# A four-layer vision network on one core: weights scaled later, heads loaded earlier, norms reordered, and GRU inputs in two fp16 parts

## The reference, cut to what matters

```python
# layer 0: retention (12 heads of 8 channels)
x = x + dwconv3x3(x)
xn = layer_norm(x, ln1_g, ln1_b)
o = softmax(rotate(xn @ q_w) @ rotate(xn @ k_w * scaling).T + mask) @ (xn @ v_w)
x = x + ((o + dwconv5x5(v)) @ out_w + out_b)
h = gelu(layer_norm(x, ln2_g, ln2_b) @ fc1_w + fc1_b)
x = x + ((h + dwconv3x3(h)) @ fc2_w + fc2_b)

# layer 1: four GRUs over the 1024 tokens of an image (two forward, two backward)
xn = layer_norm(x, ln_g, ln_b)
x_inner, z = split(xn @ w_in.T)            # 192 and 192 channels
def step(hprev, gxt):                      # gxt = x_inner @ wih.T + bih
    gh = hprev @ whh.T + bhh
    r = sigmoid(gxt[:, :h] + gh[:, :h])
    z = sigmoid(gxt[:, h:2*h] + gh[:, h:2*h])
    n = tanh(gxt[:, 2*h:] + r * gh[:, 2*h:])
    return (1 - z) * n + z * hprev
x = x + (silu(sum of the GRUs) * silu(z)) @ w_out.T

# layers 2 and 3: norm, projection, 3x3 convolution, four decaying scans,
# norm, projection, norm, MLP; twice
```

## Time and profile before

| what | value |
|---|---|
| median of three runs | 3178.32 us (3177.25 to 3181.61) |
| the profiled execution's own time | 3182.78 us |
| its span in the trace | 3181.1 us |
| busy over the span: PE, PE weight loads, DVE | 2994.2, 2308.5, 2536.2 us |
| busy over the span: ACT, POOL | 1746.1, 1063.9 us |
| mean granted TensorE clock | 0.722 of full speed |

### The profile page before, as it was taken

How to read it: one execution, slowest core, us unless ns; L and a number is a source line. 1 busy time by engine, 2 the same in 40 slices (tenths; PEclk the granted TensorE clock), 3 DMA queues, 4 the chain that set the end, 5 groups by cost and what they waited for, 6 DMA issues and landing times. The chain is left out here.

```text
span 3181.1 us, 127160 instructions
## 1 busy us (share of the span) xinstructions
PE 2994.2 (94%) x50436; PEld 2308.5 (73%) x50436; DVE 2536.2 (80%) x12120; ACT 1746.1 (55%) x5568; POOL 1063.9 (33%) x2520
## 2 busy tenths in 40 slices
PE   6799999999969989999999999999999999789987
PEld 3365665556624459999999999999999999366654
DVE  6799999999956678888888888888888888688772
ACT  2599999999912244444444444444444444344443
POOL 2377787777710022222222222222222222000000
PEclk8899999999989965555555555555555555689998
DMA  2323233232230000000000000000000000000000
GB/s 64 97 92 118 93 117 118 91 118 96 84 91 20 12 2 4 4 4 4 4 4 4 4 4 4 4 4 4 4 4 4 4 4 4 1 1 1 1 6 15
DMA packets 48219, 104.75 MB, mean 33 GB/s; under 512 B 11306, under 2 KB 18794, under 8 KB 47693
## 3 DMA queue, kind: packets, MB, share of 16 engines
q1 hardware_dynamic: 31308, 42.78, 4.8%
q0 software_dynamic: 13824, 50.34, 4.4%
q10 hardware_dynamic: 2560, 4.35, 0.5%
HBM read 84.06 MB, written 13.37 MB: 31 GB/s over the span
## 5 line engine op out<-in xcount | busy, mean ns | idle before, releaser
L578 PE MATMUL g_zr<-g_hp,g_wp 97*128 97x4 f16 x24576 | 1070.6, 171 | 3.3 <-DVE g_hp L630 3.3
L578 PEld LDWEIGHTS g_zr<-g_hp,g_wp 97*128 97x128 f16 x24576 | 945.2, 107 | 87.9 <-DVE g_hp L630 4.9
L668 ACT ACTIVATE g_e<-g_n 96x8 f32<-96x8 f32 x2048 | 355.4, 174 | 562.2 <-DVE g_n L617 562.2
L630 DVE TENSOR_TENSOR_SCAN g_hp<-g_gates,g_e 96x16 f16<-96x16 f32 x2048 | 383.8, 187 | 258.6 <-ACT g_e L668 179.4
L556 PE MATMUL g_zr<-s_inner,g_wi 96*128 96x64 bf16 (+1 forms) x6144 | 571.2, 234 | 3.1 <-DVE g_hs L605 3.1
L665 ACT ACTIVATE g_gates<-g_zr 96x16 f32<-96x16 f32 x2048 | 397.9, 194 | 243.5 <-PE g_zr L578 243.5
L585 PE MATMUL g_n<-g_hp,g_wp 97*128 97x8 f16 x8192 | 520.2, 174 | 0.0
L938 DVE CUSTOM_DVE_ANT_0 a_negated<-a_scores,a_mask 128x1024 f32<-128x1024 f32 x384 | 468.3, 1220 | 62.3 <-PE a_scores L856 61.8
L964 ACT ACTIVATE a_probs<-a_negated,a_negmax 128x1024 f32<-128x1024 f32 x384 | 442.3, 1152 | 18.4 <-DVE a_negmax L938 8.7
L886 PEld LDWEIGHTS a_turned<-a_ident,a_probs 128*128 128x128 f32 x3072 | 357.8, 141 | 93.7 <-ACT a_probs L964 3.5
L617 DVE TENSOR_TENSOR_SCAN g_n<-g_gates,g_n 96x24 f32<-96x24 f32 x2048 | 422.4, 206 | 2.3 <-ACT g_gates L665 2.3
(11 more groups left out here) (317 smaller groups left out, 3513.7 us busy)
## 6 DMA issues: line engine op xcount, KB each, us to landing
a_mask<-in_L_mask POOLq DMA_DIRECT2D x96, 512.0 KB, 5.3
a_k<-k_rows SPq DMA_DIRECT2D x96, 144.0 KB
a_q<-q_rows SPq DMA_DIRECT2D x96, 72.0 KB
o_parts<-a_o_sb SPq DMA_DIRECT2D x384, 18.0 KB
o_part<-o_parts SPq DMA_DIRECT2D x16, 192.0 KB
o_part<-o_parts ACTq DMA_DIRECT2D x16, 192.0 KB
q_rows<-r_parts SPq DMA_DIRECT2D x12, 192.0 KB
k_rows<-r_parts SPq DMA_DIRECT2D x4, 576.0 KB, 3.6
```

Of the source, the lines that this page charges most:

```text
L578: mm = pe.matmul(zr_bank[u, k][:, 1 - g, d, :, at], wp[0:97, part, (2 * u + d) * NG + g, :], hp[u][0:97, d * NB:(d + 1) * NB, e], start=False,
L630: ve.tensor_tensor_scan(flat(hp[u][0:C]), keep, flat(e1[u][:, :, :]), 0.0, ALU.mult, ALU.subtract).then_inc(h1_ok[u], 1)
L668: act.activation(e1[u][:, :, 0], tn[u, k][:, :, 2], ACT.Tanh, scale=to_tanh).then_inc(n_and_zh[u], 1)
```

## The change

Four things are changed at once.

The **norms** get an order in which image 3's mean and centring come earlier; `factor` is a list of tiles, so that images 1 and 2 spread into the mean's tiles and no longer wait for the scaling of the image before. The second and third shifts move behind the roots.

The **inputs of the GRUs** are split in two fp16 parts in place of three bf16 parts, and `PRODUCTS` has 3 pairs in place of 6. So that fp16's range does, the input is scaled by a power of two `of_x`, found in `down_and_gates` from the norm's gain and offset and the sizes of `w_in`; the weights' scale takes the largest input weight into account too. The recurrent weights keep their two fp16 parts.

The **weights of layers 2 and 3** are scaled (`ema.scale_weights`) at the start of the recurrence block, ahead of `scan_matrices`, and no longer ahead of the split.

The **parts of image 0** are loaded at the end of attention, into the four `first_masks` buffers, ahead of the last three groups' stores in SP's queue; these buffers live until the joining is done, and the joining loads images 1 to 3 alone.

```diff
 layernorm:
+        factor = [factor, mean[0], mean[1], factor]
             def spread_out(b):
                 pe.wait_ge(split, 4 * (b + 1))
-                if b:
-                    pe.wait_ge(scaled, b)
+                if b in (1, 2):
+                    pe.wait_ge(centered, b + 2)
+                if b == 3:
+                    pe.wait_ge(scaled, 1)
...
             average_of(2)
             variance_of(0)
+            average_of(3)
             variance_of(1)
             spread_out(0)
-            average_of(3)
             variance_of(2)
...
             invert(0)
+            centre(3)
             invert(1)
             scale(0)
-            centre(3)
             invert(2)
...
             root(1)
-            shift(0)
             square(3)
             root(2)
+            shift(0)
+            root(3)
             shift(1)
-            root(3)
             shift(2)
             shift(3)

-PRODUCTS = ((0, 0), (0, 1), (1, 0), (1, 1), (0, 2), (2, 0))
+PRODUCTS = ((0, 0), (0, 1), (1, 0))
+REACH = 9.85

 down_and_gates, ScalarE:
-            act.activation(magnitude, whole, ACT.Abs).then_inc(absolute, 1)
+            act.activation(gain_size[:, :], gates["gain"][:, :], ACT.Abs).then_inc(absolute, 1)
+            act.activation(offset_size[:, :], gates["offset"][:, :], ACT.Abs).then_inc(absolute, 1)
+            act.activation(w_in_size[:, :], w_in[:, 0:2 * C], ACT.Abs).then_inc(absolute, 1)
+            act.activation(magnitude[0][0:C + 1], whole, ACT.Abs).then_inc(absolute, 1)
+            act.activation(magnitude[1][:, :, :], wih[1][:, :, :], ACT.Abs).then_inc(absolute, 1)
+            act.wait_ge(magnitude_read, 1)
+            act.activation(magnitude[0][0:C], wih[0][:, :, :], ACT.Abs).then_inc(absolute, 1)
...
-            for k in range(2):
-                act.wait_ge(rest0, k + 1)
-                act.activation(wi[0:K[k], k, 1, :, 0:C], rests[k][:, :, :], ACT.Copy).then_inc(part1, 1)
 TensorE:
+                        pe.wait_ge(reached, 1)
+                        for m in range(2):
+                            mm = pe.matmul(bound[:, m:m + 1], w_in_size[:, m * C:(m + 1) * C], reach[:, :],
+                                           start=(m == 0), stop=True, skip_group_check=True)
+                        mm.then_inc(bounded, 1)
+                    if b == 0 and k == 1:
+                        pe.wait_ge(reduced, 3)
...
 VectorE:
+            ve.tensor_reduce(row_max[0:C + 1, 0:1], magnitude[0][0:C + 1], AX.XY, ALU.max).then_inc(magnitude_read, 1)
+            ve.tensor_reduce(row_max[:, 1:2], magnitude[1][:, :, :], AX.XY, ALU.max).then_inc(reduced, 1)
+            ve.tensor_reduce(row_max[0:C, 3:4], bound, AX.X, ALU.max).then_inc(reduced, 1)
+            ve.tensor_reduce(row_max[0:C, 2:3], magnitude[0][0:C], AX.XY, ALU.max).then_inc(reduced, 1)
+            add(0)
...
+            add(2)
             for k in range(2):
                 ve.wait_ge(part0, k + 1)
-                ve.tensor_tensor(rests[k][:, :, :], wih[k][:, :, :], wi[0:K[k], k, 0, :, 0:C],
-                                 ALU.subtract).then_inc(rest0, 1)
-            add(2)
-            for k in range(2):
-                ve.wait_ge(part1, k + 1)
-                ve.tensor_tensor(wi[0:K[k], k, 2, :, 0:C], rests[k][:, :, :], wi[0:K[k], k, 1, :, 0:C], ALU.subtract)
+                ve.tensor_tensor(wi[0:K[k], k, 1, :, 0:C], wih[k][:, :, :], wi[0:K[k], k, 0, :, 0:C], ALU.subtract)

 gru_phase, VectorE:
+            ema.scale_weights(ve)
             ema.scan_matrices(ve)

 attention, SP:
             heads(sp, body)
+            sp.wait_ge(maxed, (NH - 1) * CHUNKS_PER_HEAD + 16)
+            sp.wait_ge(o_out[0], 64 * (NH * GROUPS_PER_HEAD // 2 - 1))
+            for half in range(2):
+                for j in range(4):
+                    sp.dma_start(first_parts[j][:, half, :], o_parts[:, half, 0, j, 0:8, :]).then_inc(first_parts_in, 16)

 joining of the heads:
-                for b in range(NB):
+                for b in range(1, NB):
                     for j in range(4):
-                        eng.dma_start(part[b][:, j, half, :], o_parts[:, half, b, j, 0:8, :]).then_inc(loaded[b], 16)
+                        eng.dma_start(part[b][j][:, half, :], o_parts[:, half, b, j, 0:8, :]).then_inc(loaded[b], 16)
...
+                first_half(0)
                 ve.wait_ge(norm_in, 16 * 2 * NB)

 project_and_split, ScalarE:
-                    act.activation(parts(h, b)[0], product[h][:, :], ACT.Copy).then_inc(part0, 1)
-                for h in range(2):
-                    act.wait_ge(rest0, 2 * b + h + 1)
-                    act.activation(parts(h, b)[1], y[:, h, cols(b)], ACT.Copy).then_inc(part1, 1)
+                    act.activation(parts(h, b)[0], product[h][:, :], ACT.Identity, scale=by).then_inc(part0, 1)
 GpSimd:
-            po.memset(inner[C:C + 2, 1, 0, :, :], 1.0)
-            po.memset(inner[C:C + 2, 1, 1:3, :, :], 0.0)
+            po.memset(inner[C:C + 2, 1, 0, :, :], 1.0).then_inc(ones_ok, 1)
+            po.memset(inner[C:C + 2, 1, 1, :, :], 0.0)
+            po.wait_ge(ones_ok, 1)
+            po.tensor_scalar(inner[C:C + 2, 1, 0, :, :], inner[C:C + 2, 1, 0, :, :], of_x[C:C + 2, 0:1].bitcast(F), None,
+                             ALU.mult)
 VectorE:
-            ema.scale_weights(ve)
...
-                    ve.tensor_tensor(y[:, h, cols(b)], product[h][:, :], parts(h, b)[0],
-                                     ALU.subtract).then_inc(rest0, 1)
-                for h in range(2):
-                    ve.wait_ge(part1, 2 * b + h + 1)
-                    ve.tensor_tensor(parts(h, b)[2], y[:, h, cols(b)], parts(h, b)[1], ALU.subtract)
+                    ve.scalar_tensor_tensor(parts(h, b)[1], product[h][:, :], by, parts(h, b)[0], ALU.mult,
+                                            ALU.subtract).then_inc(split, 1)
```

More of the change, by code:

```diff
@@ L1314, in retention_block @@
                             lepe, lepe_w)
-        attention(nc, d["L0_mask"], first_masks, first_mask_in, q_rows, k_rows, vt, o_parts, vpad, lepe, lepe_w)
-        values.close()
+        first_parts = [t[0:C, :].rearrange("c (f t) -> c f t", f=2) for t in first_masks]
+        attention(nc, d["L0_mask"], first_masks, first_mask_in, q_rows, k_rows, vt, o_parts, first_parts, first_parts_in,
+                  vpad, lepe, lepe_w)
         gates = gate_tiles(nc, gates_ctx)
+        gates.update(gain=v["L1_ln_g"], offset=v["L1_ln_b"])
         recycle(nc)
@@ L1323, in retention_block @@
             sem = lambda name: ctx.enter_context(semaphore(nc, "o_" + name))
-            part = [sb(f"part{b}", [C, 4, 2, BANK]) for b in range(NB)]
+            later_parts = {b: sb(f"part{b}", [C, 4, 2, BANK]) for b in range(1, NB)}
+            part = [first_parts] + [[later_parts[b][:, j] for j in range(4)] for b in range(1, NB)]
             total = [sb(f"total{i}", [C, 2, BANK]) for i in range(2)]
@@ L1451, in project_and_split @@
         product = [ctx.enter_context(nc.psum_tensor(f"s_in_product{m}", [C, L], F)) for m in range(4)]
-        ready, part0, rest0, part1, gated = map(sem, ("in_ready", "part0", "rest0", "part1", "gated"))
+        ready, part0, split, gated, ones_ok = map(sem, ("in_ready", "part0", "split", "gated", "ones_ok"))
+        by = of_x[0:C, 0:1].bitcast(F)
         block = ctx.enter_context(nc.Block())
-        parts = lambda h, b: [inner[0:C, h, p, b, T:T + L] for p in range(3)]
+        parts = lambda h, b: [inner[0:C, h, p, b, T:T + L] for p in range(2)]
         @block.tensor
```

149 lines of the change are left out of this document (93 added, 56 removed).

## The result

Beside runs of the kernel before on the same chip, the changed kernel took 3144.84 us (median of 4, 3138.49 to 3149.84) where the kernel before took 3179.97 (median of 4): a ratio of 0.9889, 95% interval 0.9868 to 0.9910, about -35 us. A second comparison on another occasion gave 3151.15 us (5 runs) beside 3179.35 (19 runs): 0.9916, interval 0.9903 to 0.9928, about -28 us. The forecast was -26.3. One program thus gave 7 us more on one occasion than on the other, and the two intervals overlap only between 0.9903 and 0.9910. The profile of the first comparison is of its shortest run (3138.49 us, span 3136.8), so a second profile of each kernel stands beside it.

The account below looks back on a forecast made before the run. It took the recurrence's loop, not TensorE, as the bound there, and block savings elsewhere as going straight into the span: -10.0 + 1.0 - 13.2 - 5.0 + 0.3 + 0.6 = -26.3, from 3178.32 to 3152.0 us, range 3144 to 3159.

Parts of the forecast that it names:

- Rival (a): Recurrence: TensorE is the bound, so 4608 fewer projections give -226 us, about 2926; chance 2%.
- (b): Recurrence: sparser projections make state matmuls restart from idle; at 0.05 us a step the time is 3203; chance 2%.
- Split, -10.0: Split of the input: without the scaling, VectorE starts early and TensorE runs through; gain 10.0 us.
- Rival (c): Split: GpSimd's work holds VectorE after all, gain 0 to 5 in place of 10, 3157 to 3162; chance 8%.
- Scaling at the start, +1.0: Start of the recurrence: twelve small VectorE instructions, 3.4 us against 2.3 of cover; cost 1.0 us with a semaphore.
- Norms, -13.2: Three norms: new order keeps VectorE busy; gains 4.5, 4.5 and 4.2 us, ends -11 and -15.
- The run-through: Norms: the new order worked through with the trace's durations, 16.0 us from first inverse to end of last shift.
- Early heads, -5.0: Joining of the heads: image 0's parts already there, TensorE's last groups setting the end; gain 5.0, worst 3, best 7.
- The term of one drawn-out VectorE addition (+0.8): Joining: VectorE's sum of the last image's parts slowed because GpSimd's ran first, counted once, +0.8.
- Rival (d): Joining bound by TensorE, so early loads give nothing, and third norm stays at the low clock: 3158; chance 10%.
- (e): The change does not do what it says, its form being norms at half their gain: 3158; chance 3%.
- Gates' weights, +0.6: Gates' weights block: TensorE stops once about 0.4 us, plus two tiny products; cost 0.6, ends 0 and +3.

Follow-up runs that it names:

- the three parts timed alone: The kernel before with one part each: norms' new order, ratio 0.9936; first image's parts loaded early, 0.9988; small weights scaled at the recurrence's start, 0.9956.
- the missing products: The kernel before with three of the six products left out, still of bf16, the output lacking their share: ratio 0.9972.

## Why the prediction was right, point by point

The forecast of 3152.0 us was 7 over the first median and 1 over the second. All blocks came out near their forecast size, but the joining did so in part by luck.

- **What bounds the recurrence.** The step that carried the most, that TensorE's 100 of 100 us is no limit, held: half the projections gone, the period was 1.5113 and 1.5135 us, and with them gone alone 1.5135, where the kernel before has 1.5133 and 1.5140. Rival (a), -226 us, is out, and (b) as well. Of the rule of the Trainium skill that I had weighed there (Perfetto Trace Analysis, Identifying the Most-Contended Engine) I used one half, weight-load busy time; the page names it together with MFU, the share of the peak FLOP/s, which I didn't work out. The half that I used would have misled: weight loads fell from 94.63 to 84.52 of 100 us and the step hardly changed.
- **Split, -10.0: -9.6.** The pause was the scaling, and the scaling was held by the memset, shown by four kernels (the scaling moved, the memsets held, the two-input form, the scaling put back). Rival (c), that GpSimd's work holds the subtraction, is out; the product took 10.99 us (12 estimated). What I had not seen is why one instruction was held and its neighbours were not.
- **Scaling at the start, +1.0: +0.84.** As worked out. But my sentence that TensorE being ready earlier is of no use was true only of this placement: with the scaling elsewhere the fewer projections give 2.5 there against the kernel before, and 3.0 if some matrices go too.
- **Norms, -13.2: -13.8.** The run-through gave 16.0 us from first inverse to end, the trace 15.97. In the third the saving was 4.9 by the means of the pairs, but that leans on the one norm of before whose fold ran at 1.2 GHz; over all seven profiles of either order (means 26.7 and 22.4) it is 4.3, close to the 4.2 taken.
- **Early heads, -5.0: -5.9 (-6.8 alone).** The size was near, the path to it was not. I read waits for the loads off the first two images and let TensorE's last groups set the end. In the kernel before, VectorE already worked without a gap from 907.14 on, and in the changed one it does so from its first multiplication, while TensorE's last projection waits for VectorE (0.51 and 1.38 us). The 7.1 us between landings was also the first gap alone: in the same profile GpSimd's later additions, which start as the parts land, follow after 6.1 and 5.3. The term of one drawn-out VectorE addition (+0.8) fell on GpSimd in one profile and on VectorE in the other. Landings still set part of the end in two of the seven profiles with the early loads (38.9 and 40.8 us), where image 2's parts came 8.3 and 8.4 us after image 1's and VectorE then waited 2.7 us for GpSimd's addition. Over the seven joinings with the old loads (40.7 to 47.8 us) and the seven with the new (35.6 to 40.8) the means differ by 5.8, but the spread within each is 5 to 7. Attention's +0.3 can't be seen in its 804 to 809 us. Rival (d) is out, and so is (e), which had the norms at half their gain.
- **Gates' weights, +0.6: +0.8.**
- **The error that the range needed.** The bounds of "recurrence +-1" and "medians +-2" were too narrow. The period's level is worth up to 5.4 us, the last layers 8.7, by execution, and 10.7 us of the first profile's gain lie in these two. The first median came out at 3144.84, at the edge of the range, and that it stayed inside is luck; that the same spread moved this median is likely, but a profile shows one execution alone.

Open: the three parts timed alone and the missing products come by their ratios to -20, -4, -14 and -9 us, and by their blocks to -11.6, -6.8, -8.2 and -2.5; three of the four are larger than their blocks, and together they are larger than the whole change. Whether a program's own layout favours a level of the period I could not tell from one profile each.

## What to carry to other kernels

An engine that is busy for all of a stretch may only be filling someone else's wait: look for the one place where the filling is missing, and compare the pace. Before GpSimd is given a long memset or product, look at which of VectorE's instructions beside it are of the quick one-input form in SBUF (here the scalings, not the reductions); a 0.3 us scaling cost 7 to 11 us here, and moving it, holding the memset or using a slower form all cured it. And where a loop has levels of its own, take a second profile before explaining a few microseconds.

## What the runs showed of the hardware that I had not expected

- The recurrence's loop over four engines ran at mean periods of 1.5113 (once), 1.5133 to 1.5140 and 1.5166 us (three times), mostly held for a whole execution (once 1.5157, a mixture), and one program had 1.5166 in one execution and 1.5134 in the next.
- GpSimd's product of 2x4224 fp16 took 10.99 us, three times its memset of the same tile (3.61): 2.6 ns an element of a partition, with 2 partitions in use.
- VectorE's scaling of 96x192 with one input took 0.31 to 0.32 us free, 3.75 beside a memset of 3.73, 7.27 beside one of 7.25, and a pair of 96x96 took 10.97 beside the product of 11.16: it waits for the whole of it. Reductions and two-input instructions beside the same memsets were not held (0.34 to 0.44 us; 0.41 to 0.61 for the scalings and 1.21 for the subtractions).
